# Thirteen one-hot fields, padded tables, all rows buffered, two samples per gram matmul

## The reference

```
e = stack([tbl_f[ids[:, f]] for f in range(26)], axis=1)     # 512 x 26 x 128
T = concat([r_dense[:, None, :], e], axis=1)                  # 512 x 27 x 128
Z = einsum('bnd,bmd->bnm', T, T)                              # a gram matrix per sample
z = Z[:, upper triangle]                                      # 351 pairs
h = relu(concat([z, r_dense]) @ W_top1 + b_top1)              # 479 -> 512
h = relu(h @ W_top2 + b_top2)                                 # 512 -> 256
y = h @ W_top3                                                # 256 -> 1
```

## Time and profile before

| | us |
|---|---|
| median of three timed executions | 159.62 |
| span of the profiled execution | 187.1 |
| PE busy | 120.2 |
| ACT busy | 86.8 |
| DVE busy | 78.1 |
| POOL busy | 73.3 |
| first lookup matmul starts | 9.47 |
| first gram matmul starts | 90.76 |
| last gram matmuls start | 165.49 |

### The profile page before, as it was taken

One profiled execution on the slowest core, in us unless ns is written; L12 is line 12 of the kernel. 1 busy time (PEld: TensorE's weight loads), 2 busy tenths in 40 slices (PEclk: granted clock), 3 DMA queues, 4 the chain that ended last, 5 costly groups with the idle time before them and its releaser, 6 DMA issues.

```text
span 187.1 us, 2116 instructions
## 1 busy us (share of the span) xinstructions
PE 120.2 (64%) x644; PEld 99.2 (53%) x644; DVE 78.1 (42%) x244; ACT 86.8 (46%) x234; POOL 73.3 (39%) x82
## 2 busy tenths in 40 slices
PE   6177829612259582499930369289979999898910
PEld 6043416401138451367820359279968898787900
DVE  3242534511078170565000463449268931695410
ACT  2224254820267460896400466449568952693000
POOL 5787778777400008737787447700000000002000
PEclk9999999985558999579995556969999999999985
DMA  2554444544213795421212102210001000000000
GB/s 45 143 156 142 157 154 153 178 156 158 62 30 116 211 204 167 147 76 42 60 56 55 43 14 56 56 27 4 0 13 4 4 13 1 0 4 13 0 0 0
DMA packets 7906, 13.64 MB, mean 73 GB/s; under 512 B 2640, under 2 KB 4616, under 8 KB 7768
## 3 DMA queue, kind: packets, MB, share of 16 engines
q1 hardware_dynamic: 5528, 8.78, 15.3%
q0 software_dynamic: 2368, 4.74, 9.9%
HBM read 13.27 MB, written 0.00 MB: 71 GB/s over the span
## 4 chain that ended last, share of the span: by engine, by line
PE 29%; DMA 26%; another core or an unknown queue 17%; DVE 12%; ACT 7%; issue 3%; SPq 1%; ACTq 0%; DVEq 0%
DMA table<-tbl 26%; PE gr L356 9%; DVE Zt L410 7%; PE l L342 4%; PE l L307 4%; PE l L344 3%; DVE Zlow L404 3%; PE l L392 3%; PE tp L330 3%; ACT Zt L410 2%; PE l L301 2%; ACT XT L488 2%; DVE hot L521 2%; PE gr L307 1%
## 5 line engine op out<-in xcount | busy, mean ns | idle before, releaser
L290 POOL DMA_INDIRECT rows<-tbl,idx x72 | 71.2, 988 | 49.0 <-PE tp L330 23.3
L342 PE MATMUL l<-hot,t_hi 125*128 125x512 f32 x68 | 35.3, 519 | 34.3 <-ACT hot L451 12.8
L356 PE MATMUL gr<-XT 128*128 128x104 f32 x256 | 35.3, 299 | 19.1 <-issue 14.7
L356 PEld LDWEIGHTS gr<-XT 128*128 128x128 f32 x256 | 33.6, 214 | 21.4 <-issue 19.2
L342 PEld LDWEIGHTS l<-hot,t_hi 125*128 125x128 f32 x68 | 16.1, 237 | 47.3 <-ACT t_hi L424 24.1
L521 DVE TENSOR_SCALAR hot<-ids_bc,rownum 125x512 fp32r<-125x512 int32 x51 | 22.3, 486 | 26.9 <-remote 15.2
L344 PE MATMUL l<-hot,t_lo 125*128 125x512 f32 x68 | 32.4, 477 | 0.0
L410 ACT COPY Zt<-gr 17x24 f32<-17x24 f32 (+3 forms) x128 | 24.9, 195 | 1.7
L410 DVE COPY Zt<-gr 17x24 f32<-17x24 f32 (+3 forms) x128 | 24.8, 194 | 2.0
L404 DVE COPY Zlow<-gr 14x112 f32<-14x112 f32 x32 | 11.1, 348 | 34.6 <-remote 20.4
L424 ACT CAST t_hi<-table 125x1024 fp32r<-125x1024 f32 (+3 forms) x10 | 9.2, 916 | 33.6 <-DMA table<-tbl 27.4
(11 more groups left out here) (31 smaller groups left out, 66.1 us busy)
## 6 DMA issues: line engine op xcount, KB each, us to landing
ids_bc<-ids_oh SPq DMA_DIRECT2D x8, 250.0 KB
table<-tbl SPq DMA_DIRECT2D x4, 500.0 KB
table<-tbl SPq DMA_DIRECT2D x2, 625.0 KB
rows<-tbl,idx POOLq DMA_INDIRECT x72
w_sb<-w SPq DMA_DIRECT2D x1, 1024.0 KB
table<-tbl SPq DMA_DIRECT2D x2, 312.5 KB
w_sb<-w SPq DMA_DIRECT2D x1, 512.0 KB
table<-tbl SPq DMA_DIRECT2D x2, 187.5 KB
```

The costliest lines, as they stand in the source:

```text
L290: nc.gpsimd.indirect_dma_start(rows[:, t % ROW_TILES, place - FIRST, :], None, tbls[f], bass.IndirectOffsetOnAxis(ap=idx[:, t, f:f + 1], a ...
L342: nc.tensor.matmul(lookup_bank(i), t_hi[:, i % PARTS, c * D:(c + 1) * D], hot[:, k % HOTS, :], start=c == 0, stop=False)
L356: last = nc.tensor.matmul(gr[:, halves % 2, q, :, 0:FIELDS], XT[:, b:b + SAMPLES, :].rearrange("d s n -> d (s n)"), XT[:, b:b + SAMPLES, 1 ...
```

## The change

It touches nearly every stage:

- `ONEHOT` has thirteen fields instead of eight; all of the new ones have 1,250 rows, so there are 118 chunks instead of 68. The tables come padded to 128 partitions (`OH_ROWS = P`), laid out by the host as 128 x (8 or 10 x 128). ACT makes every fifth one-hot instead of every fourth. Two table buffers instead of three.
- PE counts `hot_used` up once per four chunks (`GROUP`). Three fields' banks are copied to `XT` by one instruction (`LOOKUPS`), with six banks of PSUM in `work`, which the grams and layers use later.
- Thirteen fields are gathered instead of 18, in four groups a tile, with buffers for all four tiles, so that POOL waits for no transposition. Tiles 0 to 2 are transposed among the lookups (`ROWS_AFTER`).
- The dense input comes transposed from the host; DVE copies it to place 0, and layer 1 reads it directly.
- A gram matmul takes two samples (`COUPLE`): stationary 64 columns, moving 52. A tile has two halves of 64 samples, so each copy is twice as long and there are half as many.
- Layer 2 gives its outputs on partitions, and layer 3 is a matmul of its own, so that a tile's result is one row of 512 bytes. The small moves to `Zt` are two DMAs of one partition each.
- For the last tile, ACT shares the relus of layer 1 and 2. The last two grams of tile 3 come before both halves of layer 1 of tile 2. The warm-up has 24 transposes instead of 16. ACT issues the first DMA of table 0.

```diff
-ONEHOT = [4, 5, 6, 12, 16, 23, 2, 9]
+ONEHOT = [4, 5, 6, 12, 16, 23, 2, 9, 11, 13, 14, 15, 18]
-OH_ROWS = 125
-OH_CHUNKS = [SIZES[f] // OH_ROWS for f in ONEHOT]
+OH_ROWS = P
+OH_CHUNKS = [-(-SIZES[f] // OH_ROWS) for f in ONEHOT]
-TABLES = 3
-DENSE_AFTER = 4
+TABLES = 2
+IDS = 3
-ACT_EVERY = 4
-ROWS_AFTER = {K_OH - 3: [0, 1], K_OH - 2: [2, 3, 4]}
+GROUP = 4
+ACT_EVERY = 5
+ROWS_AFTER = {3: [(0, 0), (0, 1)], 4: [(0, 2), (0, 3)], 6: [(1, 0), (1, 1)], 8: [(1, 2), (1, 3)], 10: [(2, 0), (2, 1)],
+              12: [(2, 2), (2, 3)]}
-ROW_TILES = 2
+ROW_TILES = TILES
+LOOKUPS = 3
+LOOKUP_BANKS = 2 * LOOKUPS
-HALVES = 4
+HALVES = 2
+COUPLE = 2
+GRAM_BANKS = 4
-WARM_UP = 16
+WARM_UP = 24
...
+    steps += [("gram", 0, 0), ("gram", 0, 1), ("gram", 1, 0), ("gram", 1, 1), ("layer1", 0, 0),
+              ("layer1", 0, 1), ("layer2", 0, 0), ("gram", 2, 0), ("layer3", 0, 0),
+              ("gram", 2, 1), ("layer1", 1, 0), ("layer1", 1, 1), ("rows", 3, 0), ("rows", 3, 1), ("layer2", 1, 0),
+              ("rows", 3, 2), ("rows", 3, 3), ("layer3", 1, 0)]
+    steps += [("gram", 3, 0), ("gram", 3, 1), ("layer1", 2, 0), ("layer1", 2, 1), ("layer1", 3, 0), ("layer2", 2, 0),
+              ("layer1", 3, 1), ("layer3", 2, 0), ("layer2", 3, 0), ("layer3", 3, 0)]
...
-            for i, f in enumerate(ONEHOT):
+            for i in range(K_OH):
                 n = OH_CHUNKS[i]
                 if i >= TABLES:
                     sp.wait_ge(lo_ready, split_parts(i - TABLES, MOST))
...
                     sp.dma_start(table[:, i % TABLES, c0 * D:c1 * D],
-                                 source[:, c0 * D:c1 * D]).then_inc(table_in[i] if part == 0 else tail_in[i], 16)
+                                 small[i][:, c0 * D:c1 * D]).then_inc(table_in[i] if part == 0 else tail_in[i], 16)
...
-                    sp.dma_start(out[t * P:(t + 1) * P, :], y[:, t:t + 1]).then_inc(y_out, 16)
+                sp.dma_start(out[t * P:(t + 1) * P, :].rearrange("p o -> o p"), y[:, t, :]).then_inc(y_out, 16)
...
-                    if t >= ROW_TILES:
-                        pool.wait_ge(tp_full, banks_filled(("rows", t - ROW_TILES, g)))
...
                     for q in range(QH):
-                        b = t * P + SAMPLES * (i * QH + q)
-                        last = nc.tensor.matmul(gr[:, halves % 2, q, :, 0:FIELDS],
-                                                XT[:, b:b + SAMPLES, :].rearrange("d s n -> d (s n)"),
-                                                XT[:, b:b + SAMPLES, 1:PLACES], start=True, stop=True)
+                        for s in range(0, SAMPLES, COUPLE):
+                            b = t * P + (i * SAMPLES + s) * QH + COUPLE * q
+                            last = nc.tensor.matmul(gr[PAD * s:PAD * (s + COUPLE), halves % HALVES, q, 0:COUPLE * FIELDS],
+                                                    XT[:, b:b + COUPLE, :].rearrange("d s n -> d (s n)"),
+                                                    XT[:, b:b + COUPLE, 1:PLACES], start=True, stop=True)
...
             for s in samples:
-                first, end = columns(s)
-                last = copy(Zlow[:, t % 2, :, first:end:SAMPLES].rearrange("n m q -> n q m"),
-                            gr[PAD * s:PAD * s + LOW, half, :, s, 0:LOW])
+                first = h * SAMPLES * QH + s // COUPLE * COUPLE * QH + s % COUPLE
+                end = first + COUPLE * QH - 1
+                last = copy(Zlow[:, t % 2, :, first:end:COUPLE],
+                            gr[PAD * s:PAD * s + LOW, half, :, column(s):column(s) + LOW].rearrange("n q m -> n m q"))
...
-                    act.wait_ge(hot_used, first_hot(i + 1))
-                    nc.scalar.copy(XT[:, :, 1 + i], lookup_bank(i)).then_inc(lookup_copied, 1)
+                    if ends_lookups(i):
+                        act.wait_ge(hot_used, groups_used(first_hot(i + 1)))
+                        first = LOOKUPS * lookup_group(i)
+                        nc.scalar.copy(XT[:, :, 1 + first:2 + i],
+                                       lookup_banks(i).rearrange("p f b -> p b f")).then_inc(lookup_copied, 1)
...
+                        dve.wait_ge(dense_in, 16)
+                        nc.vector.tensor_copy(XT[:, :, 0], dense_t[:]).then_inc(dense_copied, 1)
+                        nc.vector.memset(XT[:, :, PLACES:PAD], 0.0).then_inc(xt_ready, 1)
...
+                    for v in range(PIECES if t < TILES - 1 else 1):
+                        nc.vector.tensor_scalar(h2[:, v, :], l2_block(t, v), tail_sb[:, 0, v:v + 1], 0.0,
+                                                ALU.add, ALU.max).then_inc(h2_ready, 1)
+                elif kind == "layer3":
+                    dve.wait_ge(l3_full, t + 1)
+                    nc.vector.tensor_copy(y[:, t, :], l3_row(t)).then_inc(y_ready, 1)
```

More of the change, by code:

```diff
@@ L92, in timeline @@
         steps.append(("onehot", 0, i))
[L93 to L104, removed]
+        steps += [("rows", t, g) for t, g in ROWS_AFTER.get(i, [])]
+    steps += [("gram", 0, 0), ("gram", 0, 1), ("gram", 1, 0), ("gram", 1, 1), ("layer1", 0, 0),
[4 more added lines that the diff above has]
+              ("layer1", 3, 1), ("layer3", 2, 0), ("layer2", 3, 0), ("layer3", 3, 0)]
     return steps
@@ L138, in hots_made, with dlrm_tower @@
     return sum(by_scalar(x) == scalar for x in range(k + 1))
-def dlrm_tower(nc, dense, ids, ids_oh, tbls, w1, w2, b2, w3, out):
+def dlrm_tower(nc, dense, ids, ids_oh, tbls, small, w1, w2, tail, out):
     f32, f32r, i32 = mybir.dt.float32, mybir.dt.float32r, mybir.dt.int32
@@ L320, in _ @@
                     banks += 1
-                if kind == "dense":
-                    pe.wait_ge(dense_in, 16)
-                    for j in range(TILES):
-                        last = nc.tensor.transpose(tp[:, bank, j * P:(j + 1) * P], dense_sb[:, j, :], ident[:])
-                    last.then_inc(tp_full, 1)
-                elif kind == "rows":
+                if kind == "rows":
                     a, n = GROUPS[i]
@@ new lines, in _ @@
+                    for v in range(PIECES):
+                        for u in range(BLOCKS):
+                            if by_both(t, u):
+                                pe.wait_ge(h1_act, units_ready(t, u))
+                            else:
+                                pe.wait_ge(h1_ready, units_ready(t, u))
+                            last = nc.tensor.matmul(l2_block(t, v), w2_sb[:, u, v * P:(v + 1) * P],
+                                                    h1[:, u, :], start=u == 0, stop=u == BLOCKS - 1)
@@ new lines, in _ @@
+                    last.then_inc(l2_full, 1)
+                elif kind == "layer3":
+                    pe.wait_ge(h2_ready, PIECES * t + (1 if t == TILES - 1 else PIECES))
+                    if t == TILES - 1:
+                        pe.wait_ge(h2_act, 1)
+                    for v in range(PIECES):
+                        last = nc.tensor.matmul(l3_row(t), tail_sb[:, 1, v:v + 1], h2[:, v, :], start=v == 0,
+                                                stop=v == PIECES - 1)
+                    last.then_inc(l3_full, 1)
@@ L406, in copy_gram @@
             last.then_inc(low_copied, 1)
             for s in samples:
-                first, end = columns(s)
+                first = h * SAMPLES * QH + s // COUPLE * COUPLE * QH + s % COUPLE
+                end = first + COUPLE * QH - 1
                 for g, n in enumerate(HIGH_ROWS):
-                    last = copy(
-                        Zt[PAD * g:PAD * g + n, :, t * P + first:t * P + end:SAMPLES].rearrange("n c q -> n q c"),
-                        gr[PAD * s:PAD * s + n, half, :, s, n - CHUNKS:n])
+                    last = copy(Zt[PAD * g:PAD * g + n, t, :, first:end:COUPLE],
+                                gr[PAD * s:PAD * s + n, half, :, column(s) + n - CHUNKS:column(s) + n].rearrange("n q c -> n c q"))
```

234 lines of the change are left out of this document (135 added, 99 removed).

## The result

The changed kernel takes **130.88 us** in the median of four executions (129.14 to 131.58), beside 160.28 for the kernel before (159.22 to 161.3, four executions). The ratio is 0.814, with a 95% interval of 0.806 to 0.821: 29 us faster. The forecast was 137 us, range 128 to 156.

What follows compares the result with a forecast made beforehand. The prediction took the lookups to wait for tables whose transfers use about five of 16 DMA engines. A (lookups, up to the first gram) 77.5 + B (grams and tower) 59.5 = 137 us, range 128 to 156.

Steps and rivals of the forecast that it cites:

- B: Grams and tower, from the first gram on: 44.6 us to the last gram plus 14.9 after it, 59.5 (79.3 before).
- Tables spread: Table transfers in the lookups: 128 rows use 16 DMA engines instead of five, 50 us where 110 GB/s would take 101.
- Stage A by the balance of engines: Lookups up to the first gram: four engines at 56 to 59 us, ACT last, 0.56 a chunk, 77.5 us in all.
- POOL's end at 69 us: Gathers on POOL: 52 at 0.99 us with 0.30 of issue between them end near 69 us, POOL waiting for no tile.
- The clock: PE at the start of the lookups: the first six chunks at 0.86 us add 2.4 us, then the clock rises.
- Gram slot: Each two-sample gram instruction on PE: 0.058 us, between 0.055 and 0.111; 3.7 us per 64 samples, 29.7 in all.
- Copies: Gram copies: 2.7 to 3.0 us per 64 samples, 23 in all, below PE's 3.7; three-field lookup copy 2.1 us.
- The result's transfer: End of the kernel: the result as one 512-byte row lands in 2.2 us instead of 7.2, plus 0.8 for issue and end.
- Long pieces without a releaser: Profile of the kernel before: six waits with no known cause, 32.1 us together; 27.5 us of span left out.
- Rival 1: Grams: slots don't shrink, a fixed price of 0.111 us per weight load; 27 us more, 164 in all; chance 0.10.
- Rival 2: Lookups: ACT's one-hots behind copies hold PE, then tables come late; 0.70 a chunk, +16.5, 153.5 us; chance 0.13.
- Rivals 3 and 4: Lookups: padding doesn't spread transfers (chance 0.05), or the clock stays at 1.2 GHz (0.04); each 170 us in all.

Runs made afterwards that it cites:

- a_125rows_2: The changed kernel with tables and one-hots on 125 partitions instead of 128: 171.74 us, ratio 1.073 to the kernel before.
- b_padded_2: The kernel before with only its eight tables padded to 128 partitions: fastest two executions 131.14 and 132.72 us, ratio 0.823.
- a_same: The changed kernel as it is, run again on another chip: fastest two executions 126.0 and 126.4 us, beside 160.9 for the kernel before.
- a_couples_apart: The changed kernel with gram matmuls reordered, 16 on the lower output partitions, then 16 on the upper: 146.3 to 149.5 us, 0.056 a slot.
- b_couples_2: The kernel before with only its four-sample gram matmul cut into two of two samples: 157.99 us, ratio 0.981.
- the first set: The first runs of several follow-up kernels, sharing one chip on which the kernel before took 182 to 191 us; their times are not used.
- b_direct: The kernel before with plain transfers of fixed rows in place of the gathers: 161.64 us, ratio 1.005.

## Why the prediction was right, and where not

The forecast held (137 against 130.88, inside the range, the first mechanism). The miss of 6 us is the sum of misses of both signs: A +2.2, B up to the end of the last gram -10.1 (34.5 us where 44.6 were forecast), tail +0.1 (15.0 and 14.9), and +1.9 around the span, for which the sum had no term. So part of the closeness is luck. By its steps:

- **Tables spread.** Right, and the largest part. Less than five engines' worth of a 16-engine share was the row that decided. *a_125rows_2* and *b_padded_2* show it from both sides: without it the change is 7% slower, alone it is 18% faster. The rule that the prediction takes from the Trainium skill (DMA: Bandwidth & Descriptors, "Why a DMA increments its semaphore by 16 and not by 1") agrees with both, the share being 0.44 with 125 rows and, in the stretches shown, 0.75 to 0.93 with 128.
- **Stage A by the balance of engines.** Nearly right: 77.5 predicted, 79.7 in the first trace and 75.0 in *a_same*. PE did its 118 chunks and the transposes between 6.5 and 78.8 us with 5.6 us of one wait; without it 0.565 a chunk, where I had 0.56. That the two agree is partly luck. I had ACT as last in line, with 6 us of waits and dispatch gaps; in the trace PE runs at its own pace (10.00 of 10 us busy from 20 to 30) and waits 2.3 us in all for ACT's one-hots and 2.0 for another gather. (The 12 row groups hold 39 transposes and not 48, 1 us less.) The start at 6.5 us was forecast at 6.8.
- **POOL's end at 69 us.** Wrong: it ended at 85.9. I took the mean of the kernel before, 0.99 us a gather, and it became 1.28. See below for why. This step was called no bound and is one, in this kernel together with PE. It was missing among the rivals.
- **The clock.** The first chunks were forecast at 1.2 GHz. They came at 0.23 a matmul, the full clock, behind 24 transposes of warm-up instead of 16 with only 0.4 us of idle time between instead of 4.3: 2.4 us less. No run tells which of the two did it. The fall of the clock behind the wait for gathers took about 1 us back.
- **Gram slot.** The term that was most mis-sized: 0.058 us against 0.031 measured, 512 of them 14 us less of PE work. I had bounded it from below by half a slot, 0.055, and left out that two could overlap; *a_couples_apart* shows that they do. The 62 ns set beside it there are twice the measured slot. Not all 14 us came through: between the first and the last gram PE waits 4.2 us, where I had taken 2 (1.3 for the copies, 1.8 for the moves of tile 0, 1.1 for relus).
- **Copies.** 2.7 to 3.0 us a half forecast, 2.5 measured. I had scaled with the slope between copies of other layouts; in the new order of dimensions twice the elements cost hardly more, though no run tells order from size. The three-field copy took 1.73 us, 2.1 forecast. Shorter copies, by *b_couples_2*, are the part without which the grams would have brought 3 us. With them, 16 x 2.4 = 38 us of copies became 8 x 2.5 = 20.
- **The result's transfer.** Right in kind: 7.2 us from issue to landing before; now the last product is copied at 127.5 to 127.8 us and the span ends at 129.2, 1.4 us later, where I had 3.0 (2.2 and 0.8). The views have no landing time for it. The 1.6 us gained were lost on PE before it, 13.5 us from the last gram to that copy instead of 11.9.
- **Long pieces without a releaser.** I left 27.5 us of the profiled span out of the sum. The clean trace of the old code confirms it: A is 83.3 (80.3 taken), B 77.2 plus 1.9 around the span (79.3 taken).
- **Rivals.** Rival 1 fell: slots shrank by more than half. Rival 2 had the right kind of cause, an engine that supplies PE, but named ACT, which held PE 2.3 us; the gathers did for 7.6, and not 16. Rivals 3 and 4 fell.

What the sum did not show is that thirteen fields are too many. It gave each engine's total for this kernel and stopped there; the same table of totals for eight and eleven fields would have had POOL's line fall as PE's rises.

## What to carry to other kernels

A transfer's share of the DMA engines tells more than its rate: a share that stays just under a fraction such as 5/16, as the 0.28 here, while other transfers reach 0.99, is a reason to look at the outer dimension; one constant mended 34 us of this kernel's lookups. When a unit of work can go to either of two engines, as a field here to gathers or to one-hots, sum both engines' lines for several splits, not only for the one proposed. A faster stage is worth what the next bound leaves: grams at 0.6 of the price gave 3 us where the copies behind them stayed.

## What the runs showed of the hardware that was not expected

- **Gathers beside two-input work of DVE.** In the changed kernel's trace, the 11 gathers that overlap a subtraction of DVE (L578) by 0.5 us or more take 1.89 us in the mean, the 7 that run while DVE is idle 0.97. Over all 52, a line fitted to the overlaps gives about 0.7 us more per us of L578 and about 0.3 per us of one-hots (L593). The rows show it, POOL's and DVE's timelines of the same time:

```profile
52.31 2.29 POOL L331 DMA_INDIRECT rows<-tbl,idx  x1 [0.30 <-issue]
...
65.59 0.94 POOL L331 DMA_INDIRECT rows<-tbl,idx  x1 [0.30 <-issue]
```

```profile
51.80 1.49 DVE L578 TENSOR_TENSOR t_lo<-table,t_hi 128x1280 fp32r<-128x1280 f32 x1
53.20 2.46 DVE L593 TENSOR_SCALAR hot<-ids_bc,rownum 128x512 fp32r<-128x512 int32 x6
...
63.14 0.47 DVE L593 TENSOR_SCALAR hot<-ids_bc,rownum 128x512 fp32r<-128x512 int32 x1
69.77 0.89 DVE L593 TENSOR_SCALAR hot<-ids_bc,rownum 128x512 fp32r<-128x512 int32 x2 [6.16 <-PE work L382]
```

  At 65.6 us DVE is idle and the gather takes 0.94; at 52.3 it runs beside L578 and takes 2.29. Full DMA engines alone do not do it: the gather at 64.34 takes 0.95 us while DVE is idle and the DMA share is 0.97 (64.3 to 65.3 us). So a kernel that fills DVE with such work seems to slow its own gathers. That the one causes the other is read from traces and was not tried by an experiment of its own. The Trainium skill (SBUF — State Buffer, "Who interferes with whom") describes one pair of ports that DVE and GpSimd share under an exclusive lock, taken by a DVE instruction with two SBUF inputs against a GpSimd instruction that reads SBUF. L578 has two such inputs, and its overlaps here agree with that in kind; whether a gather counts as such a reader isn't shown.

- **PE in steps.** On the chip of the first set, and in the profiled execution of the kernel before, PE at times goes on only in steps while nothing is shown that it waits for. The layout of the changed kernel is not free of it on that chip: such pieces add up to 34 us in the chain of *a_125rows* and to 7 in that of *a_couples_apart*. The timeline of PE in *b_couples* there:

```profile
92.95 0.21 PE L357 MATMUL gr<-XT 128*64 128x52 f32 x1 [0.39 <-issue]
93.67 0.28 PE L357 MATMUL gr<-XT 128*64 128x52 f32 x2 [0.51 <-issue]
95.78 0.46 PE L357 MATMUL gr<-XT 128*64 128x52 f32 x4 [1.84 <-issue]
97.88 0.46 PE L357 MATMUL gr<-XT 128*64 128x52 f32 x3 [1.64 <-issue]
```

  The starts are 0.7 or 2.1 us apart. In the traces of the kernel before, *b_padded* and *b_couples*, each run of such pieces ends within 5 us of the end of a run of gathers on POOL; in *a_125rows* the last ends 5.3 us behind it. *b_direct* was meant to tell whether the gathers cause them, but ran on a chip without them, and so did *a_same*, meant to tell how the changed kernel fares with them. Their cause stays open.
